# A mixture-of-experts stage with lists in blocks of 128 rows, read by tiles of 256 rows through registers, and its first tile set ahead of the late lists

## What is computed

```python
n = layernorm(x)                              # 4096 rows of 128
logits = n @ gate_w + gate_b                  # 8 experts
top2, weights = softmax over the two best     # TOP_K = 2
y = sum over the two of weight * (silu(n @ w1[e]) * (n @ w3[e])) @ w2[e]   # hidden size 512
x = x + layernorm(y)
```

## Time and profile before

| | us |
|---|---|
| median of three executions | 1286.84 |
| the profiled execution, its own time | 1282.15 |
| its span, first to last instruction | 1280.3 |
| state-space layer ends, mixture of experts starts | 1005.7, 1006.9 |
| first list written | 1039.9 |
| first product of the first tile | 1054.0 |
| last product of the last tile | 1239.4 |
| end of the last scatter's issue | 1246.8 |
| end of the span | 1280.3 |

### The profile page before, as it was taken

One profiled execution on the slowest core, in us unless ns is written; L12 is line 12 of the kernel. 1 busy time (PEld: TensorE's weight loads), 2 busy tenths in 40 slices (PEclk: granted clock), 3 DMA queues, 4 the chain that ended last, 5 costly groups with the idle time before them and its releaser, 6 DMA issues. The chain is left out here.

```text
span 1280.3 us, 16672 instructions
## 1 busy us (share of the span) xinstructions
PE 1076.7 (84%) x4978; PEld 545.3 (43%) x4978; DVE 982.0 (77%) x1338; ACT 734.6 (57%) x1167; POOL 697.4 (54%) x599
## 2 busy tenths in 40 slices
PE   6654679999999996979898989889888849999864
PEld 2211224444444442324333333333343538888763
DVE  5996866575664645999999999999988386776645
ACT  6774444555645446667585857665654535555445
POOL 0001442151431201788899888998887136777774
PEclk8886889999999998999999999999989969999996
DMA  6000000000000002222232322222221011111225
GB/s 232 1 1 0 0 1 1 1 2 1 0 0 0 1 1 75 83 91 88 84 106 69 103 71 102 68 73 74 67 66 41 33 57 43 54 52 53 53 53 198
DMA packets 32553, 67.08 MB, mean 52 GB/s; under 512 B 5760, under 2 KB 5952, under 8 KB 32256
## 3 DMA queue, kind: packets, MB, share of 16 engines
q1 hardware_dynamic: 27056, 55.16, 13.2%
q0 software_dynamic: 4992, 10.23, 3.0%
q10 hardware_dynamic: 432, 0.76, 0.2%
HBM read 56.57 MB, written 9.57 MB: 52 GB/s over the span
## 5 line engine op out<-in xcount | busy, mean ns | idle before, releaser
L1801 POOL TENSOR_TENSOR prod<-hs,csb 128x1024 f32<-128x1024 f32 x128 | 301.8, 2358 | 145.6 <-DVE hs L1848 143.7
L1848 DVE TENSOR_TENSOR_SCAN hs<-dA,carry,pD 128x512 f32<-128x512 f32 x256 | 313.8, 1267 | 5.2 <-DVE pD L1861 0.8
L1557 PE MATMUL pY<-prod,const 128*128 128x512 f32 x512 | 245.7, 603 | 1.8 <-POOL prod L1801 1.8
L1707 ACT ACTIVATE dA<-dt,negA 128x512 f32<-128x512 f32 x256 | 168.0, 714 | 17.3 <-POOL dt L1770 15.8
L1861 DVE TENSOR_TENSOR pD<-dtu,pD 128x1024 f32<-128x1024 f32 x128 | 155.7, 1216 | 12.3 <-PE pD L1571 12.3
L1557 PEld LDWEIGHTS pY<-prod,const 128*128 128x128 f32 x512 | 96.9, 193 | 117.0 <-issue 112.2
L2330 POOL DMA_INDIRECT g<-moe_rows,source x78 | 75.7, 970 | 57.0 <-DVE source L2526 33.5
L1028 ACT ACTIVATE stage<-pR,vec 128x512 f32<-128x512 f32 x64 | 43.9, 687 | 100.1 <-PE pR L728 99.9
L2577 DVE SCALAR_TENSOR_TENSOR pR<-pR,silu 128x512 f32<-128x512 f32 x78 | 54.5, 699 | 58.2 <-ACT silu L2290 58.2
L2347 POOL DMA_INDIRECT moe_outs<-y,to x78 | 76.9, 986 | 29.9 <-issue 22.2
L2069 PE MATMUL pR<-x,moe_hi 128*128 128x256 f16 x312 | 86.3, 277 | 3.0 <-DVE x L2563 2.8
(11 more groups left out here) (454 smaller groups left out, 2571.6 us busy)
## 6 DMA issues: line engine op xcount, KB each, us to landing
csb<-ssm_c SPq DMA_DIRECT2D x128, 256.0 KB, 3.1
raw<-moe_w SPq DMA_DIRECT2D x12, 512.0 KB, 4.8
room<-moe_outs SPq DMA_DIRECT2D x8, 512.0 KB, 7.9
hidw<-hid_w SPq DMA_DIRECT2D x1, 2048.0 KB, 9.9
moe_rows<-g SPq DMA_DIRECT2D x8, 256.0 KB, 2.0
outT<-X SPq DMA_DIRECT2D x8, 256.0 KB, 2.1
X<-xT SPq DMA_DIRECT2D x3, 512.0 KB, 4.1
g<-moe_rows,source POOLq DMA_INDIRECT x78, 2.5
```

Source lines behind the costliest of these rows:

```text
L1557: last = nc.tensor.matmul(YB[c][:], G.ident, prod[:, slot(b, n), c, :], start=n == 0, stop=n == DST - 1)
L1707: last = nc.scalar.activation(dA[:, slot(b, n), c, :], dt[:, b, c, :], ACT.Exp, scale=negA[:, c, n:n + 1])
L1801: nc.gpsimd.tensor_tensor(prod[:, slot(b, n), :, :], hs[:, slot(b, n), :, :], csb[:, slot(b, n), :, :].to_broadcast([P, CB, N]), ALU.mult)\
L1848: last = nc.vector.tensor_tensor_scan(hs[:, slot(b, n), c, :], dA[:, slot(b, n), c, :], dBu(n, c), carry[:, b, n, c:c + 1], ALU.mult, ALU.add)
```

## The change

The lists are padded to 128 rows for each expert instead of 256: COLS becomes 71, with 16 early and 55 late. Tiles still hold 256 rows of one expert, and there are still 39 of them. So a tile's two blocks are no longer at fixed places of the list: where an expert has an odd number of blocks, the second half of its last tile reads a block of the next expert. From the counts DVE works out for each tile its first block and, by a bit mask, the places of its two blocks in the rings (`slot_x`, `slot_y`); PE reads two of these words into registers for each tile before it turns the rows, and ACT reads two for each tile before it puts the results away, now with two instructions of 128 columns instead of one of 256. If a half tile is not the one that a block belongs to, what it writes is overwritten by a later tile before the block is scattered: the scatter of block c waits for tile (c + 7) // 2.

POOL gathers and scatters single blocks, 24 ahead, from a ring of 32, with a result ring of 16. PE turns the first tile and starts its products ahead of the late lists, of which it does one quarter before the first `up`, one after it and two after the second. DVE copies the first tile's rows between the quarters, and the late `sources` and `targets` stay where they are, after all quarters and ahead of the loop.

In the state-space phase the scores of the first SCORED = 5 groups are taken out of the last slice and put at the end: two ahead of the final projection, one ahead of the final variance, two after it, with one ACT copy for all; the filler products of the tail (`keep_busy`) go. The last state's product, the gating and the last residual sum move to DVE.

The core of the diff (semaphore names, buffers and the SP's waits are left out):

```diff
-SCORED = 4
+SCORED = 5
...
@@ phase_ssm, PE @@
+            def next_score(i):
+                pe.wait_ge(S["next_normed"], i + 1)
+                for j in range(N // P):
+                    c = i * N // P + j
+                    last = nc.tensor.matmul(DD[:, 0, c * E:(c + 1) * E], G.normed[i][:, j * P:(j + 1) * P], G.gatew[:, :],
+                                            start=True, stop=True)
+                last.then_inc(S["next_scores"], 1)
...
-                    if is_last(t, b) and n in SCORE_AT:
-                        next_score(SCORE_AT.index(n))
...
-            keep_busy(10)
-            for step in range(2):
-                tail(NT - 1, B - 1, step)
-                keep_busy((3, 10)[step])
+            pe.wait_ge(G.gate_loaded, 16)
+            for i in (0, 1):
+                next_score(i)
+            tail(NT - 1, B - 1, 0)
+            next_score(2)
+            tail(NT - 1, B - 1, 1)
+            for i in range(3, SCORED):
+                next_score(i)
...
@@ phase_ssm, DVE @@
-            tail(NT - 1, B - 1, 0)
+            nc.vector.tensor_tensor(prod[:, slot(b, n), :, :], hs[:, slot(b, n), :, :],
+                                    csb[:, slot(b, n), :, :].to_broadcast([P, CB, N]), ALU.mult).then_inc(S["prod_last"], 1)
+            dve.wait_ge(S["acc"], state(t, b, n))
+            for c in range(CB):
+                last = nc.vector.tensor_tensor(ygate[:, c, :], YB[c][:], sgate[b][:, c, :], ALU.mult)
+            last.then_inc(S["ygated"], 1)
+            tail(t, b, 0)
+            dve.wait_ge(S["scaledC"], at(t, b))
+            nc.vector.tensor_tensor(X[:, b, ds(t)], X[:, b, ds(t)], scaled[:, b, :], ALU.add).then_inc(S["addedC"], 1)
...
@@ phase_moe @@
-    COLS = 2 * TILES
+    COLS = (PAIRS * P + E * (P - 1)) // P
-    GRID = B * T // ROWS
-    AHEAD, GR, HR, YR, UPS = 8, 8, 4, 4, 3
+    GRID = B * T // P
+    GRID2 = B * T // ROWS
+    AHEAD, GR, HR, YR, UPS = 24, 32, 4, 16, 3
+    WASTE = E - 1
...
+        def last_tile_of(c):
+            return min((c + WASTE) // 2, TILES - 1)
...
+            def slot_of(i, r):
+                return pe.value_load(slot_x[0:1, r, i:i + 1], min_val=0, max_val=GR - 1)
             def x_turn(i):
-                pe.wait_ge(S[f"gathered{i % GR}"], 32 * (i // GR + 1))
+                for c in (2 * i, 2 * i + 1):
+                    if c < COLS and (c % 2 or c == COLS - 1):
+                        pe.wait_ge(S[f"gathered{c // 2 % (GR // 2)}"], landed(c))
                 if i >= 1:
                     pe.wait_ge(S["x_in"], i)
-                for w in range(2):
-                    for r in range(2):
+                for r in range(2):
+                    at = slot_of(i, r)
+                    for w in range(2):
                         last = nc.tensor.matmul(XG[:, (2 * w + r) * P:(2 * w + r + 1) * P],
-                                                g[:, i % GR, r, w * P:(w + 1) * P], ident16[:, :], start=True, stop=True)
+                                                g[:, bass.ds(at, 1), w * P:(w + 1) * P].rearrange("p a d -> p (a d)"),
+                                                ident16[:, :], start=True, stop=True)
                 last.then_inc(S["x_turned"], 1)
...
             pe.wait_ge(S["expert"], 1)
+            pe.wait_ge(S["slots"], 2)
             es = {0: expert_of(0)}
             x_turn(0)
+            list_late(0)
             for n in range(UNITS):
                 i, u = divmod(n, 2)
                 up(n, es[i])
+                if n == 0:
+                    list_late(1)
+                if n == 1:
+                    list_late(2)
+                    list_late(3)
...
@@ phase_moe, ACT @@
             def put_y(i):
                 act.wait_ge(S["down"], 2 * i + 2)
-                nc.scalar.activation(y[:, i % YR, :, :].rearrange("p r d -> p (r d)"), Y[:, i % 2, 0:2 * P], ACT.Copy,
-                                     scale=1.0 / WS).then_inc(S["y_out"], 1)
+                for r in range(2):
+                    at = act.value_load(slot_y[0:1, r, i:i + 1], min_val=0, max_val=YR - 1)
+                    last = nc.scalar.activation(y[:, bass.ds(at, 1), :].rearrange("p a d -> p (a d)"),
+                                                Y[:, i % 2, r * P:(r + 1) * P], ACT.Copy, scale=1.0 / WS)
+                last.then_inc(S["y_out"], 1)
...
@@ phase_moe, POOL @@
+            def scatter(c):
+                pool.wait_ge(S["to"], lists(c))
+                pool.wait_ge(S["y_out"], last_tile_of(c) + 1)
+                nc.gpsimd.indirect_dma_start(outs, bass.IndirectOffsetOnAxis(ap=to[:, c:c + 1], axis=0),
+                                             y[:, c % YR, :], None).then_inc(S[f"scattered{c // 2 % (YR // 2)}"], 16)
...
+            for c in range(AHEAD):
+                gather(c)
+            for c in range(COLS):
+                scatter(c)
+                if c + AHEAD < COLS:
+                    gather(c + AHEAD)
...
@@ phase_moe, DVE: behind past and expert_f, ahead of expert @@
+            nc.vector.tensor_tensor(past[:, :, :], past[:, :, :], odd[:, :].unsqueeze(1).to_broadcast([1, TILES, E]), ALU.mult)\
+              .then_inc(S["missed"], 1)
+            dve.wait_ge(S["missed"], 1)
+            nc.vector.tensor_reduce(skip_f[:, :], past[:, :, :], AX.X, ALU.add).then_inc(S["skip_f"], 1)
+            dve.wait_ge(S["skip_f"], 1)
+            for r in range(2):
+                nc.vector.scalar_tensor_tensor(out=first_f[:, r, :], in0=double[0:1, r, :], scalar=1.0, in1=skip_f[:, :],
+                                               op0=ALU.mult, op1=ALU.subtract).then_inc(S["first_f"], 1)
+            dve.wait_ge(S["first_f"], 2)
+            nc.vector.tensor_copy(first_i[:, :, :], first_f[:, :, :]).then_inc(S["first_i"], 1)
+            dve.wait_ge(S["first_i"], 1)
+            for slots, ring in ((slot_x, GR), (slot_y, YR)):
+                nc.vector.tensor_scalar(slots[:, :, :], first_i[:, :, :], ring - 1, None, ALU.bitwise_and).then_inc(S["slots"], 1)
...
             for q in range(1, QUARTERS):
                 column(hot_late, slice(q * QP, (q + 1) * QP), SOON, LATE, col_p)
+                if q == 2:
+                    take_x(0)
                 pair(hot_late, slice((q - 1) * QP, q * QP), LATE, q + 1, lane_p)
```

More of the change, by code:

```diff
@@ L1753, in _ @@
             tiles(act, body)
-            for step in (2, 0, 1):
+            for step in (0, 1):
                 tail(NT - 1, B - 1, step)
+            act.wait_ge(S["next_scores"], SCORED)
+            nc.scalar.activation(G.scored[:, :], DD[:, 0, 0:SCORED * N // P * E], ACT.Copy).then_inc(S["next_scored"], 1)
         @block.gpsimd
@@ L2047, in late, with landed, stored @@
             return i - EARLY
+        def landed(c):
+            return 16 * len([d for d in range(c + 1) if d // 2 % (GR // 2) == c // 2 % (GR // 2)])
+        def stored(c):
+            return 16 * len([d for d in range(c + 1) if d // 2 % (YR // 2) == c // 2 % (YR // 2)])
+        def last_tile_of(c):
+            return min((c + WASTE) // 2, TILES - 1)
         @block.sync
@@ L2135, in _, with list_late @@
             last.then_inc(S["listed"], 1)
-            for q in range(QUARTERS):
+            def list_late(q):
                 pe.wait_ge(S["hot_part"], q + 2)
@@ L2325, in _, with lists @@
             nc.gpsimd.iota(spare[:, :], [[P, COLS]], base=P * PAIRS + PAIRS, channel_multiplier=1).then_inc(S["lanes"], 1)
-            def gather(i):
-                if i >= GR:
-                    pool.wait_ge(S["x_turned"], i - GR + 1)
-                for r in range(2):
-                    nc.gpsimd.indirect_dma_start(
-                        g[:, i % GR, r, :], None, rows,
-                        bass.IndirectOffsetOnAxis(ap=source[:, 2 * i + r:2 * i + r + 1], axis=0))\
-                      .then_inc(S[f"gathered{i % GR}"], 16)
+            def lists(c):
+                return 1 if c < SOON else 2
@@ L2454, in _ @@
             steps = lane_f[:, 0:GRID].unsqueeze(1).to_broadcast([P, E, GRID])
-            nc.vector.scalar_tensor_tensor(out=grid[:, :, :], in0=steps, scalar=float(ROWS),
+            nc.vector.scalar_tensor_tensor(out=grid[:, :, :], in0=steps, scalar=float(P),
                                            in1=counts.unsqueeze(2).to_broadcast([P, E, GRID]),
@@ L2571, in hid_low_part @@
                   .then_inc(S["hid_low"], 1)
-            take_x(0)
             for n in range(UNITS):
```

167 lines of the change are left out of this document (88 added, 79 removed).

## The result

The changed kernel took 1326.45 us (median of four executions, 1323.18 to 1329.56), the kernel before 1286.78 beside it: a ratio of 1.0316 over all these executions, 95% interval 1.0279 to 1.0353. It is slower, by 39.7 us of the medians; forecast were 1326 us and a range of 1301 to 1342.

What follows compares the result with a forecast made beforehand. POOL's DMA count and PE were taken to bound the kernel before, PE's sequencer the changed tiles. Terms −4.4 + 3.3 + 1.0 + 41.8 − 2.5 = +39.2 us, set on the median 1286.84, gave 1326 us, range 1301 to 1342.

Steps and rivals of the forecast that it cites:

- The mechanism: Tiles: PE's sequencer sets 5.8 us by its own sum; queued products don't shorten it, ACT costs nothing, POOL no bound.
- hidden loads: Rival, tiles: PE's sequencer goes on during a load, a tile stays at 4.42 us, 1274 us in all; chance 0.09.
- The falling clock: Rival, tiles: PE's idle pieces lower its clock, ten products a tile at half clock, 37 us more, 1363 us; chance 0.07.
- The tile: From `up` of tile 1 to `up` of tile 38: 37 × 5.82 = 215.3 us instead of 173.6, +41.8 us.
- issuing, 3.3 us: Tiles: time from a turn to the next first load, taken as sequencer work; only stalls on a full queue could shrink.
- 5.4 as a lower end: Tiles: cheaper loads, with addresses in one step for each pair and fewer stalls; 15.5 us less, 1310 us; chance 0.14.
- The list path: Up to the first list: +0.3 us for a grid of 256 instead of 128 numbers; nothing taken for a fallen clock.
- The start: First list to tile 1's `up`: +3.3 us for DVE's order and list steps, +1.0 us for PE's clock.
- The 1.0 us for a falling clock: Start of the tiles: PE idles some 3 us, so 1.0 us was added for a lower clock, ends 0 and 2.
- Moving the first tile forward gains nothing: Start of the tiles: the quarters only change sides, and the second tile queues behind the late lists on DVE.
- The state-space part: Last slice and tail, to the mixture's first instruction: 1.7 us back from DVE's wait, −3.0 in the tail, −4.7 us.
- The end: Tile 38's `up` to the last scatter's issue: 4.9 us behind PE's last product instead of 7.4, −2.5 us.

Runs made afterwards that it cites:

- e1: Changed kernel, but PE turns blocks from constant ring places instead of two words read into registers: 1277.2 us, 4.52 us for a tile.
- e2: Changed kernel, but ACT writes its results to constant ring places instead of reading two words for each tile: 1327.4 us, 5.93 us for a tile.
- e5: Changed kernel with PE's three loads of a tile moved a tile ahead and apart from each other: 1326.7 us, 5.89 us for a tile.
- e3: Kernel before, with the expert's word read two more times ahead of each tile's turn, values unused: 1314.2 us, 5.47 us for a tile.
- e4: Changed kernel with the three groups of filler products (10, 3 and 10) put back around the state-space tail: 1326.1 us.
- e14: Kernel before without its three groups of filler products, scores still inside the slice: 1286.6 us, ratio 1.0020.
- e7: Changed kernel with the first tile put back behind all four quarters of the late lists: 1329.3 us.
- e12: Changed kernel with one packed, untested word for a tile on PE, and a place of its own for every block: 1276.1 us, ratio 0.9933 to before.
- e13: Kernel with one packed word for a tile, plus five filler products on PE behind the last state-space scores: 1273.9 us, ratio 0.9928 to before.

## Why the prediction was right, and where it wasn't

**The mechanism held.** PE's sequencer sets the tile by a sum of its own, queued products don't shorten it, ACT's reading is free, POOL is no bound any more. e1, e2 and e5 each could have refuted one of these and didn't. Of the rivals, hidden loads (1274 us) needed tiles at 4.42, and the row at 1104.59 with its 0.61 us of issue answers to the earlier trace rows; in e3 PE waits out loads that its products don't need. The falling clock needed less than 1.00 between the tiles: the changed kernel has two idle times of 0.5 to 0.65 us in each tile, and the row of 1100 to 1200 has 1.00.

**The tile: 5.82 forecast, 5.93 measured** (41.8 and 45.85 us for 37). The loads were priced right (0.64 for 0.65, 0.64 and 0.74), the addresses too (2 × 0.24 for 2 × 0.25). What I called issuing, 3.3 us, is 3.23 in the tile shown (median 3.33). But I read it as issuing 48 products with possible stalls on a full queue, and kept 5.4 as a lower end for that; it is 24 register instructions and three semaphores, which the earlier trace rows (0.2 us from one to the next but one) could have told by a count. The terms as written add up to 5.80, not 5.82. PE's idle time was forecast at 1.5 to 1.9 us for a tile and is 1.1 (19 us of 100): its busy time for a tile is 4.8 us here, not 4.4.

**The list path, +0.3 forecast, +5.7 measured**, is the term that was mis-sized. The step is "the scores take their place, and if the clock fell for it the next phase's first products would lose up to 2 us"; I took nothing. The clock fell, twice for 6 us, and in e4 3.6 of the 5.7 us go with the first of these stretches and a part of the second. I had looked at the fillers as something that merely fills; e14 shows that they hold the clock, and e4 that they have their price where PE has no gap.

**The start, +4.3 forecast, +1.25 measured.** The order of events was as forecast: DVE at the late rows, then `take_x(1)`, then tile 1, 11.1 us behind tile 0. The 14 list steps took 3.85 us instead of 4.4 (the prices that I named, four at 0.5 and ten at 0.2, add up to 4.0), and three quarters of lists 0.94 and 1.72 us instead of 1.3 and 2.6: I had priced them by the earlier trace rows, 2.58 for two, over half of it at the low clock (0.50 up to 1050), but here the granted clock was 1.00 from 1053 on, behind tile 0's first products. The 1.0 us for a falling clock did not come: PE stood 3.20 us ahead of tile 1's `up`, and the clock stayed at 1.00. "Moving the first tile forward gains nothing" is off by the 1.0 us of e7.

**The state-space part, −4.7 forecast, −6.5 measured.** DVE's wait of 3.75 us became 1.97, its second one in that slice, 1.55, went too, and a third grew by 0.3: 3.0 instead of the 1.7 of the first score alone. The tail gave 3.5 instead of 3.0. DVE's rows of the changed kernel, which answer to the earlier trace rows:

```profile
950.32 1.23 DVE L1851 TENSOR_TENSOR pD<-dtu,pD 128x1024 f32<-128x1024 f32 x1 [1.97 <-PE pD L1569]
...
992.97 1.29 DVE L1904 TENSOR_TENSOR ygate<-pY,sgate 128x512 f32<-128x512 f32 x2 [2.08 <-PE pY L1555]
...
1000.54 0.69 DVE L1908 TENSOR_TENSOR X<-X,scaled 128x512 f32<-128x512 f32 x1
```

**The end, −2.5 forecast, −1.5 measured.** I counted two scatters behind the last result; there are four in a row, 1.27 us apart, since a list may be put away only when the last tile that can hold it is done: the first two wait for tile 37, and the two that wait for tile 38 queue behind them (POOL's timeline of the changed kernel, the first two of the four; the last starts at 1292.68):

```profile
1288.87 0.96 POOL L2385 DMA_INDIRECT moe_outs<-y,to  x1 [1.37 <-ACT y L2325]
1290.14 0.96 POOL L2385 DMA_INDIRECT moe_outs<-y,to  x1 [0.30 <-issue]
```

**The total.** 1326 against 1326.45 is closer than the terms deserve. They miss by 6.3 us (+45.5 for +39.2), and the stretch ahead of them was 2.0 longer in the profiled execution. I set the sum on the median of the kernel before, 4.7 above its profiled execution, while the changed kernel's median lies 3.1 below its own: 7.8 us between the two, which cancelled the miss by luck.

## What to carry to other kernels

Count what an engine's sequencer does by itself in one turn of the loop (loads of words, tests of their bounds, register arithmetic, semaphore waits), each with its distance to the next such record: if the sum is over the time of the engine's own work, it is the bound, and reordering doesn't help. An index that a loop reads on PE is dear, so read one packed word without a test; here that turns a loss of 3% into a gain of 0.7%. On an engine with slack, as ACT here, such reading can be free. When products that only fill are taken away or added, look at the granted clock of the stretch behind them, and at whether PE has a gap there.

## What the runs showed of the hardware

- On PE's sequencer a load of one word takes 0.30 us (0.36 to the next step), of three words 0.77; a test of its bounds 0.29; an address 0.125, an ALU_OP 0.112, a semaphore wait 0.105. These add up without overlap (5.88 us for a tile); 52 products with their loads of weights add some 0.6 us of that, by the estimate above.
- Products did not pass a load with its test on PE: in e3, with PE standing 1.09 us, those behind the loads start 0.05 us behind the last test, though they need nothing of what is loaded.
- The same loads on ACT, two for a tile, cost this kernel nothing (e2).
- Unpacking a word took no instruction more (e12): two of the FUSED_REGOPS that make the four addresses of a turn took 98 and 60 ns in place of 46, and one of those for the weights 96.
- The granted clock of a stretch followed on what PE did before: filler products ahead of, between and behind the tail's steps kept it at 1.00 to 1012 (e4), five behind the tail's last scores did not (e13, 0.50 from 996), and without any it fell between 998 and 1000 (e14). In the changed kernel it fell a second time at 1012 for 6 us with PE busy all the time; why is open. Idle time alone doesn't decide it: PE stood 3.20 us at 1061.36 of the changed kernel and 2.51 at the barrier of the kernel before without a fall, 2.35 at the barrier of the changed one with a fall.
